# Where fp32 weights become bf16: casting DMAs on GpSimd's queue against plain loads on SP's queue with a copy on ScalarE

## What is computed

```python
x = x + attn_a(layernorm(x), in_proj_w, conv_w, ..., out_proj_w, ...)   # in_proj, 4-tap conv, SiLU, state-space scan, gate, RMS norm, out_proj
x = x + ffn(layernorm(x), W_r, W_k, W_v, mu_r, mu_k)    # r = sigmoid(xr W_r), k = relu(xk W_k)^2, out = r * (k W_v)
x = x + attn_b(layernorm(x), w_attn, b_attn, w_proj, b_proj)   # QKV, RoPE, causal softmax attention of 16 heads, projection
x = x + ffn(layernorm(x), W_r, W_k, W_v, mu_r, mu_k)    # the same weights again
```

## Time and profile before

| | us |
|---|---|
| median of 2 timed runs | 9025.27 (9016.78 to 9033.76) |
| the profiled execution, its own time | 8989.9 |
| its span (first to last instruction, slowest core) | 8988.4 |
| spans of the 8 cores | 8953.5 to 8988.4 |

### The profile page before, as it was taken

How to read it: one execution, slowest core, us unless ns; L and a number is a source line. 1 busy time by engine, 2 the same in 40 slices (tenths; PEclk the granted TensorE clock), 3 DMA queues, 4 the chain that set the end, 5 groups by cost and what they waited for, 6 DMA issues and landing times.

```text
span 8988.4 us, 85844 instructions; the slowest of 8 cores (8953.5 to 8988.4 us)
## 1 busy us (share of the span) xinstructions
PE 4912.1 (55%) x21232; PEld 2028.9 (23%) x21232; DVE 3283.3 (37%) x6508; ACT 2352.5 (26%) x3568; POOL 149.6 (2%) x234
## 2 busy tenths in 40 slices
PE   2254664656646563444516656556666676735555
PEld 2222322323223231111102212111121221212222
DVE  3344445444444543455512323322111111113444
ACT  1122313123131231000011101224655575731111
POOL 2000000000000000000020000000000000000000
PEclk9985675756757565666657767667788888966666
DMA  8520120201102010211152222211001000012110
GB/s 156 119 75 20 45 61 4 64 11 54 58 7 64 10 55 24 52 38 38 38 98 72 69 69 67 63 43 40 19 34 34 12 23 34 1 37 50 40 40 32
DMA packets 338092, 420.00 MB, mean 47 GB/s; under 512 B 123041, under 2 KB 182946, under 8 KB 337570
## 3 DMA queue, kind: packets, MB, share of 16 engines
q1 hardware_dynamic: 248210, 360.00, 12.8%
q0 software_dynamic: 89424, 54.52, 4.0%
HBM read 331.39 MB, written 119.87 MB: 50 GB/s over the span
## 4 chain that ended last, share of the span: by engine, by line
PE 36%; DVE 23%; ACT 17%; DMA 11%; issue 10%; DVEq 1%; SPq 1%; ACTq 1%; POOL 0%; POOLq 0%
ACT pt_sb L191 11%; PE pEF L191 9%; PE pB L191 9%; PE pA L191 9%; PE pCD L191 7%; ACT D L191 3%; DVE y L191 2%; DMA xtm<-x 2%; DVE t1b L191 2%; DVEq L189 1%; DMA wtmpC<-wqkv_l 1%; ACT tr L191 1%; DVE yraw L191 1%; PE pT L191 1%; DMA mrow<-stats_h 1%
## 5 line engine op out<-in xcount | busy, mean ns | idle before, releaser
L191 ACT ACTIVATE pt_sb<-pEF,ebias 128x1024 bf16<-128x1024 f32 (+1 forms) x640 | 630.5, 985 | 820.4 <-PE pEF L191 761.9
L191 PE MATMUL pA<-pt_sb,vb 128*65 128x512 bf16 (+3 forms) x1152 | 470.7, 409 | 424.3 <-ACT pt_sb L191 290.7
L191 ACT ACTIVATE pt_sb<-pCD,ebias 128x1024 bf16<-128x1024 f32 (+2 forms) x640 | 610.1, 953 | 113.4 <-PE pCD L191 30.3
L191 DVE TENSOR_TENSOR pt_sb<-pt_sb,mask01b 128x128 bf16<-128x128 bf16 x512 | 115.3, 225 | 1405.1 <-ACT pt_sb L191 1379.1
L191 PE MATMUL pA<-r_t,wr_sb 128*128 128x512 bf16 x512 | 147.8, 438 | 676.6 <-DVE h L191 633.8
L191 PE MATMUL pB<-pt_sb,vb 128*65 128x512 bf16 (+3 forms) x1152 | 470.0, 408 | 36.5 <-DVE pt_sb L191 30.7
L191 ACT ACTIVATE D<-pEF,cumcT 128x128 f32<-128x128 f32 x512 | 188.1, 367 | 852.1 <-PE pCD L191 814.9
L191 DVE TENSOR_TENSOR Gm<-E,Gmsk 128x1024 bf16<-128x1024 f32 x128 | 156.8, 1225 | 557.0 <-ACT E L191 557.0
L191 ACT ACTIVATE sig_t<-pA 128x512 bf16<-128x512 f32 x64 | 38.2, 597 | 1141.4 <-PE pA L191 1141.4
L191 PE MATMUL pEF<-qq_sb,K_sb 64*128 64x512 bf16 (+1 forms) x1152 | 265.1, 428 | 72.1 <-DMA qq_sb<-q_hbm 71.5
L191 PEld LDWEIGHTS pA<-pt_sb,vb 128*65 128x65 bf16 x1152 | 130.4, 113 | 746.2 <-issue 740.8
(11 more groups left out here) (254 smaller groups left out, 8275.4 us busy)
## 6 DMA issues: line engine op xcount, KB each, us to landing
winm<-winb_h SPq DMA_DIRECT2D x272, 256.0 KB, 2.6
wq_sb<-wqkvb_h SPq DMA_DIRECT2D x192, 256.0 KB, 2.6
xrtB<-xres SPq DMA_DIRECT2D x16, 2048.0 KB, 8.8
xrtC<-xres SPq DMA_DIRECT2D x16, 2048.0 KB, 11.9
xtm<-x SPq DMA_DIRECT2D x32, 512.0 KB, 5.3
xres<-xcs SPq DMA_DIRECT2D x32, 512.0 KB, 4.0
xrt<-xres SPq DMA_DIRECT2D x8, 2048.0 KB, 11.2
xres<-xrt SPq DMA_DIRECT2D x8, 2048.0 KB, 6.9
```

Of the source, the lines that this page charges most:

```text
L191: ins = getattr(h, ent[1])(*ent[2], **ent[3])
```

## The change

Three edits.

1. In stage 0 the 35 chunks of `win_l` are loaded as fp32 into a new buffer `wtmpf` by SP's queue, copied to bf16 in `wtmp` by ScalarE, and stored from there by SP's queue. These instructions stand ahead of the token loop in both lists.
2. In both B stages the weights are loaded as fp32 by SP's queue through `wstg`, a ring of four chunks, and copied to bf16 by ScalarE; all of wr first, then wk, then wv. They stand ahead of the loads of group 0 in SP's list.
3. The casts of `wqkv_l` and `wproj` stay on GpSimd's queue but are issued in B1, at its start, and stage C waits for them no more (the barrier between the stages covers them).

```diff
@@ phase0 @@
         for m in range(NMCH):
...
-            w = [st[m - 2]] if m >= 2 else []
-            ldw = S.dma("gpsimd", sl, src, waits=w, ch="wr%d" % b)
-            st[m] = S.dma("gpsimd", c.winb_h[m], sl, waits=[ldw], ch="ws%d" % b)
+            w = [w_cstm[m - 2]] if m >= 2 else []
+            ldw = S.dma("sync", slf, src, waits=w, ch="wr%d" % b)
+            S.op("scalar", "copy", sl, slf,
+                 waits=[ldw] + ([st[m - 2]] if m >= 2 else []))
+            w_cstm[m] = S.ms("scalar")
+            st[m] = S.dma("sync", c.winb_h[m], sl, waits=[w_cstm[m]], ch="ws%d" % b)
@@ phaseB @@
-    for kc in range(NCH):
-        prev = []
-        for wi, (wsb, wsrc) in enumerate([(wr_sb, c.wrT), (wk_sb, c.wkT),
-                                          (wv_sb, c.wvT)]):
-            w_wld[(wi, kc)] = S.dma("gpsimd", wsb[:, kc * 1024:(kc + 1) * 1024],
-                                    wsrc[kc * 128:(kc + 1) * 128, :],
-                                    waits=prev, ch="bw%d" % kc)
-            prev = [w_wld[(wi, kc)]]
+    for k in range(24):
+        wi, kc = k // NCH, k % NCH
...
+        b = k % 4
+        sl = wstg[:, b * 1024:(b + 1) * 1024]
+        w = [w_wld[((k - 4) // NCH, (k - 4) % NCH)]] if k >= 4 else []
+        ld = S.dma("sync", sl, wsrc[kc * 128:(kc + 1) * 128, :], waits=w,
+                   ch="bw%d" % b)
+        S.op("scalar", "copy", wsb[:, kc * 1024:(kc + 1) * 1024], sl, waits=[ld])
+        w_wld[(wi, kc)] = S.ms("scalar")
     w_wl = w_wld[(2, NCH - 1)]
+    if tag == 1:
...
+        for m in range(24):
+            b = m % 2
+            sl = wtmpC[:, b * 1024:(b + 1) * 1024]
+            w = [stq[m - 2]] if m >= 2 else []
+            ldw = S.dma("gpsimd", sl, kchunk_view(c.wqkv_l[m]), waits=w,
+                        ch="qr%d" % b)
+            stq[m] = S.dma("gpsimd", c.wqkvb_h[m], sl, waits=[ldw], ch="qs%d" % b)
+        for m in range(NCH):
...
@@ phaseC @@
-    for m in range(24):
...
-        ldw = S.dma("gpsimd", sl, kchunk_view(c.wqkv_l[m]), waits=w, ch="qr%d" % b)
-        st[m] = S.dma("gpsimd", wqkvb_h[m], sl, waits=[ldw], ch="qs%d" % b)
...
-            w = ([w_win_used[gm - 3]] if gm >= 3 else []) + \
-                ([st[m]] if mg == 0 else [])
+            w = [w_win_used[gm - 3]] if gm >= 3 else []
             ld_w = S.dma("sync", wsl, wqkvb_h[m], waits=w, ch="cw%d" % b)
...
-        w = [st_q] + (w_c1done + [w_wcast, w_wcast2] if qm == 0 else []) + \
+        w = [st_q] + (w_c1done if qm == 0 else []) + \
             ([w_q_used[qm - 2]] if qm >= 2 else [])
```

More of the change, by code:

```diff
@@ L379, in phase0 @@
     st = {}
-    with nc.sbuf_tensor("wtmp", [128, 2 * NCH * 128], BF16) as wtg:
+    w_cstm = {}
+    with nc.sbuf_tensor("wtmp", [128, 2 * NCH * 128], BF16) as wtg, \
+         nc.sbuf_tensor("wtmpf", [128, 2 * NCH * 128], F32) as wtfg:
         wtmp = wtg.ap()
+        wtmpf = wtfg.ap()
         for m in range(NMCH):
@@ L384, in phase0 @@
             sl = wtmp[:, b * 1024:(b + 1) * 1024]
+            slf = wtmpf[:, b * 1024:(b + 1) * 1024]
             src = kchunk_view(c.win_l[m])
-            w = [st[m - 2]] if m >= 2 else []
-            ldw = S.dma("gpsimd", sl, src, waits=w, ch="wr%d" % b)
-            st[m] = S.dma("gpsimd", c.winb_h[m], sl, waits=[ldw], ch="ws%d" % b)
+            w = [w_cstm[m - 2]] if m >= 2 else []
[4 more added lines that the diff above has]
+            st[m] = S.dma("sync", c.winb_h[m], sl, waits=[w_cstm[m]], ch="ws%d" % b)
     c.woutb = c.stW.enter_context(nc.sbuf_tensor("woutb", [128, 16 * 1024], BF16)).ap()
@@ L1034, in phaseB @@
     w_ost = {}
+    wstg = al("wstg", [128, 4 * 1024], F32)
     w_wld = {}
-    for kc in range(NCH):
-        prev = []
-        for wi, (wsb, wsrc) in enumerate([(wr_sb, c.wrT), (wk_sb, c.wkT),
-                                          (wv_sb, c.wvT)]):
-            w_wld[(wi, kc)] = S.dma("gpsimd", wsb[:, kc * 1024:(kc + 1) * 1024],
-                                    wsrc[kc * 128:(kc + 1) * 128, :],
-                                    waits=prev, ch="bw%d" % kc)
-            prev = [w_wld[(wi, kc)]]
-    w_wl = w_wld[(2, NCH - 1)]
+    for k in range(24):
+        wi, kc = k // NCH, k % NCH
+        wsb = (wr_sb, wk_sb, wv_sb)[wi]
+        wsrc = (c.wrT, c.wkT, c.wvT)[wi]
+        b = k % 4
[5 more added lines that the diff above has]
+        w_wld[(wi, kc)] = S.ms("scalar")
+    w_wl = w_wld[(2, NCH - 1)]
+    if tag == 1:
+        c.wqkvb_h = nc.dram_tensor("wqkvb_h", [24, 128, NCH * 128], BF16,
+                                   kind="Internal").ap()
+        c.wpb_h = nc.dram_tensor("wpb_h", [NCH, 128, NCH * 128], BF16,
+                                 kind="Internal").ap()
+        wtmpC = al("wtmpC", [128, 2 * 1024], BF16)
+        stq = {}
+        for m in range(24):
[6 more added lines that the diff above has]
+        for m in range(NCH):
+            b = m % 2
+            sl = wtmpC[:, b * 1024:(b + 1) * 1024]
+            src = bass.AP(c.wproj.tensor, c.wproj.offset + m * 128,
+                          [[DM, 128], [128 * DM, NCH], [1, 128]])
+            ldw = S.dma("gpsimd", sl, src, waits=[stq[22 + m]], ch="qr%d" % b)
+            stq[24 + m] = S.dma("gpsimd", c.wpb_h[m], sl, waits=[ldw],
+                                ch="qs%d" % b)
     S.op("vector", "memset", h1, 0.0)
@@ L1270, in phaseC @@
     w_o512 = S.ms("vector")
[L1271 to L1274, removed]
-    for m in range(24):
-        b = m % 2
-        sl = wtmpC[:, b * 1024:(b + 1) * 1024]
-        w = [st[m - 2]] if m >= 2 else []
-        ldw = S.dma("gpsimd", sl, kchunk_view(c.wqkv_l[m]), waits=w, ch="qr%d" % b)
-        st[m] = S.dma("gpsimd", wqkvb_h[m], sl, waits=[ldw], ch="qs%d" % b)
[L1281 to L1290, removed]
+    wqkvb_h = c.wqkvb_h
+    wpb_h = c.wpb_h
     S.op("vector", "memset",
@@ L1583, in phaseC @@
             gm2 = qm * NCH + mo
-            w = ([w_wp_used[gm2 - 3]] if gm2 >= 3 else []) + \
-                ([st[24 + mo]] if qm == 0 else [])
+            w = [w_wp_used[gm2 - 3]] if gm2 >= 3 else []
             ld_w = S.dma("sync", wsl, wpb_h[mo], waits=w, ch="cw%d" % b)
```

## The result

| | before | after |
|---|---|---|
| median of the timed runs, us | 9030.2 (16 runs, 8987.59 to 9101.98) | 9101.1 (17 runs, 9078.11 to 9165.5) |
| ratio to before | | 1.0081, 95% interval 1.0054 to 1.0107 |
| profiled execution, us | 8989.9 | 9185.49 |

The change makes the kernel 71 us slower (the interval reaches from 49 to 97 us), which is less than 2%. The forecast of 9172 us had the sign, and the casts cost their whole length where it said they would, but one term was far too small, and the time lies 9 us under its range.

What follows compares the result with a forecast made beforehand. Stage 0 was taken as bound by its chain of 32 token tiles, each load behind the previous tile's stores on SP, not by an engine. Terms 202 + 45 + 3 - 103 = +147 us on 9025.3 gave 9172 us, range 9110 to 9250.

Steps and rivals of the forecast that it cites:

- The place of the casts: Stage 0: all 35 cast rounds stand before the first `xtm` load, their whole length on the path, 210 us.
- The round of 6.0 us: Stage 0 casts on SP: load 4.4, copy 1.0, store issue 0.4, semaphore hops 0.2; bounds 5.5 and 7.2 us.
- The relief of the token loop, 8 us: Stage 0: without casts beside it, 17 tiles take 14.23 us each in place of 14.71, 8 us saved.
- B1 +26: Stage B1: ring makes group 0's `mrow` 49 us late, less the 23.3 us `wr_sb` stall removed, 26 us longer.
- B2 +19: Stage B2: ring makes group 0's `mrow` 39 us late, less the 19.5 us `wr_sb` stall removed, 19 us longer.
- C -103: Stage C, matmul part of group 0: the wait for the rope tables goes, 103 us saved, bounds 100 to 107.
- Contention of the hoisted casts +3: Stage B1: stage C's casts contend with 2 MB loads of one or two groups, 3 us, bounds 0 to 8.
- 1 (a round of 7.2): SP queue of stage 0: cast loads land no faster on SP; +189 us, 9214 us, slower by over 2%; chance 0.15.
- 2 (the slow ring, +106): B prologue bound by DMA at the slowest 2 MB load's pace, +106 in place of +45, 9233 us; chance 0.07.
- 5 (a lower clock in the token loop): Stage 0: TensorE idles some 220 us, then the loop runs at a lower clock; +179 us, 9204 us; chance 0.03.
- Rival 4: Stage 0: casts stay hidden under the token loop, -55 us, 8970 us; chance 0.02, shared with any missed faster mechanism.
- Rival 3: Stage 0: loads overlap earlier copies and stores, round about 3.0 us; sum +42, 9067 us, not slower; chance 0.05.

Runs made afterwards that it cites:

- e5: Kernel before, with the first `xtm` load waiting for the last two stores of the `win_l` casts, which stay on GpSimd; 9201.9 us, ratio 1.0183.
- e1: Kernel before with only the stage 0 edit (`win_l` casts by SP and ScalarE ahead of the token loop); 9224.5 us, ratio 1.0163.
- e4: Kernel after with stage 0 put back as before, so only the B weights and stage C edits remain; 8942.0 us, ratio 0.9895.
- e2: Kernel before with only the B weights edit (ring on SP and ScalarE ahead of group 0's loads); 9096.6 us, ratio 1.0059.
- e3: Kernel before with only the casts of stage C moved to B1, behind its weight loads on GpSimd's queue; 8949.4 us, ratio 0.9792.
- e7: Kernel after with the load of chunk m+1 put ahead of the store of chunk m in SP's list; 9018.2 us, ratio 0.9994.
- e6: Kernel before with the `win_l` casts and `woutb` loads on GpSimd moved behind the token loop; 9178.4 us in its one run.
- e9: Kernel after with stage 0 casts as before, group 0's B loads ahead of the ring, next tile's `xtm` load ahead of this tile's stores; 8765.7 us, ratio 0.9673.

## Why the prediction was wrong

Taken by its steps:

- **The place of the casts: right.** All 35 rounds stand in front of the first `xtm` load, which comes at 211.8 us (predicted 221). e5 shows that the place alone does it.
- **The round of 6.0 us: 0.26 too long.** It measured 5.74, inside the bounds of 5.5 and 7.2. The copy took 1.04 us (predicted 1.0), the store's issue 0.4, and from the load's issue to the copy 4.2 where I had 4.4 and a semaphore hop. Over 35 rounds that is 9 us.
- **The relief of the token loop, 8 us: the term that failed.** From the first `xtm` load to stage A it measured 476.2 us in place of 511.4 as a median over the cores, a relief of 35 (40 in e1, 44 in e5), and 22 on core 3 alone (505.3 to 483.3), from 14 on core 1 to 64 on core 4. I took 14.71 us for a tile beside the casts and 14.23 for one without, both from core 3, and applied the difference to the first 17 tiles only. Both values came from the least typical core: of the eight it had the shortest tiles beside the casts and the longest without. The 14.23 was not a tile free of contention: in that stretch core 3 issued its loads 0.8 us from its neighbour's, and cores 0 and 1 of the same execution already ran at 13.1. And so the later tiles gained too. With core 0's rows the same term would have been 17 tiles by 15.69 less 13.16, 43 us. How much of the 35 is the missing casts and how much the changed offset, no run separates; at offsets of 4 us and more a tile took 14.4 to 15.7 beside casts and 12.8 to 13.2 without, so the casts are the larger part. Core 3 went to 13.59 us: 16 tiles by 1.12 are 18, 12 by 0.64 are 8, and the tile of the burst lost 4, together 22. The other cores had up to 15.7 beside the casts and came to 13.0 to 13.8. The timeline of one other core of before would have shown it.
- **B1 +26: right**, measured +27 on cores 0 to 3 (+24 in e4). `xrtB` was issued 44.7 us into the stage (predicted 45), and TensorE started at 58.3 (predicted 58). Of the slowing by the casts of C, 10 us were predicted and 10 measured (34.6 in e2, 44.7 in after). The pace of 1.6 us held (1.56 in e2), though the rows it stood on make 1.8 for each 512 KB (8.8 less 2.6 over 3.5), not 1.7.
- **B2 +19: 6 to 11 too much**; +8 in after, +11 in e4, +13 in e2. The issue of `xrtB` (35.6, predicted 35) and TensorE's start (46.0, predicted 48) were nearly as worked out. The gain subtracted for `wr_sb` was too small, and again for core 3's sake: its 19.5 us are the least of the eight, the others waited 21.5 to 23.8 us, and core 3 itself came out 17 longer in after. The same row of core 0, before:

```profile
PE pA L191 <- DMA wr_sb<-wrT: 23.3, 3, 9.8
```

What gave the other cores the rest was not followed.
- **C -103: 7 too little**, measured -110, and the wait of 113 us is gone with none in its place. **Contention of the hoisted casts +3: right**, +2.5 in e3.

The terms make +147 as predicted and +92 as measured by stages: 35 of the 55 us lie in stage 0 (27 in the loop, 9 in the rounds), 11 in B2, 7 in C, and 2 in B1, whose +27 holds the contention as well. With 35 for the loop in place of 8 the same sum would have been +120, a time of 9145 us and inside the range. The measured 9101 lies lower still, by the smaller terms and by the 21 us between stages and timed medians, which are not explained. The range was short on that side because all its bounds varied the rounds and the B ring, and the token loop had one value without bounds.

The rivals: 1 (a round of 7.2) and 2 (the slow ring, +106) did not come about. 5 (a lower clock in the token loop) did not either: the granted clock over stage 0 reads 1.00 (the upper level, 2.4 GHz) in after as before, and eight transposes take 1.01 us in both the earlier trace rows (after, core 3, in the loop):

```profile
485.11 1.01 PE L191 MATMUL pT<-idb,xnt 128*128 128x128 bf16 x8 [4.42 <-DVE xnt L191]
```

Rival 4 needed the casts hidden; the first `xtm` load at 211.8 us shows that they are not. Rival 3 (rounds of 3.0 us) was refused for the order of issue on SP. That was the right reason, since changing this order gives 3.3 us a round (e7).

The estimate by the Trainium skill, DMA: Bandwidth & Descriptors, section Anatomy of one DMA, was 168 us for the casts, a round of 4.8 us. The page gives its fit for transfers that GpSimd issues, and here SP issued them. The trace does not agree: 201 us, 5.74 a round, and the load alone lands after 4.0 us in the median of after where the fit gives 3.2. The row taken in its place (3.9 us for `xtm`) was the better guide:

```profile
wtmpf<-win_l SPq DMA_DIRECT2D x35, 512.0 KB, 4.0
```

## What to carry to other kernels

Work that leaves an unhurried queue for a busy, strictly ordered one costs its whole length where it stands, whatever engine does it; before moving it, ask what stands behind it, and issue load m+1 ahead of store m, or the second buffer does nothing. When a contention is to be taken away, read the price with it and without it on several cores, not from the slowest core of the page alone, whose work may be slow for another reason. Give a relief bounds like any other term.

## What the runs showed of the hardware that was not expected

- With no DMA of other work beside its token loop, a core's 512 KB store landed in 2.9 us (median) when the neighbouring core's loads came about 2 us apart, and in 5.2 when they nearly coincided; the 512 KB load in 4.3 against 6.0 (e6, cores 5 and 7). The offset was not set, so this is what went together, not a cause shown. A tile of the loop took 12.8 to 13.3 us at an offset of 3.2 us or more, and 14.7 to 14.8 at 0.5. Cores 6 and 7 of e6 began in step and stayed near it for all 32 tiles; with 200 us of other work ahead of the loop the pairs of after were 2 to 6 us apart.
- A casting load on GpSimd's queue and a plain load on SP's with a ScalarE copy cost the same in a ring that waits for each: 5.77 and 5.75 us from one load to the next (e5, after).
- With the DMA engines 97% busy in place of 83% (100 to 200 us, core 3), a casting load took 8.6 us as a median in e9 against 5.6 before, and an `xtm` load 8.2 against 5.5.
